# A fused two-layer graph network: order of steps in the joined projection stage, and the queues of its loads and stores

## The chip, the cores and the metric

One core of a Trainium2 chip. The metric is the device time of one execution in microseconds. A core has five engines with a queue each: TensorE (matmul), VectorE, ScalarE, GpSimd and SyncE, which here only gives out DMAs. They are ordered against each other by semaphores alone.

## The reference, cut to what matters

Two layers over 3125 nodes of 256 features and 50000 edges. The stage concerned ends the first layer and prepares the second:

```python
x = x + _L0_ffn_ref(_layernorm(x))            # two experts per node, weighted, layer-normed
xn = _layernorm(x)
x = x + _L1_gnn_ref(xn, edge_index, ...) + _L1_mix_ref(xn, ...)
# gnn: x_lin = xn @ W; a_src, a_dst = two scores per head and node; softmax over the edges of a node
# mix: rmsnorm(xn), q, k, v = x @ w_qkv; q, k = elu(.) + 1; kv = sum over nodes of k (outer) v
```

## The kernel before

Nodes lie on 125 lanes, 25 to a lane, and are worked on as 25 tiles of 125 nodes, in five groups of five tiles (`TB`, `NB`). The kernel is a row of stages with a barrier of all engines between them. The diff touches one, `stage_project1`. Two things run through it.

First the combination of the experts' rows, on VectorE for a whole group at a time: `weigh` (L1719) adds the two gathered expert rows of a node with their weights, `measure_y` and `centre_y` (L1727, L1735) norm the sum, `add_y` (L1741) adds it to x, `measure_x`, `spread_of_x` and `scales` (L1746 to L1765) give the factors of the second norm. ScalarE takes two roots (`root`, `two_roots`) and writes the normed rows (`normalise`, L1659). Each root and each following exponential needs another function table, so ScalarE loads one.

Then the projection, `project(u)` (L1674 on ScalarE, L1775 on VectorE, loop L1898 on TensorE): TensorE transposes the group's rows (L1887), ScalarE copies them (L231, L232), TensorE makes the queries of the group (L1894), VectorE and ScalarE apply the activation (L1780, L1678, L1791), and for each tile TensorE makes key and value (L1907) and the graph features and scores (L1912), VectorE the low part and the key (`low_part`, `key_of`), ScalarE the copies and the exponential (`keep_tile`), TensorE adds to the state (L1878). Products of two tiles can wait in PSUM. The steps of the next group's combination stand between those of this group's tiles in the order that VectorE's `project` and ScalarE's `project` write out by hand.

SyncE stores each finished tile of features (L1615). GpSimd gathers the expert rows (L1640, 50 of them), scatters the last 91 of 391 columns of edge records to memory (L245 by L1645), waits for them to land and tells SyncE, which loads the sorted records back (L1617). When the scores are shifted by their least value, SyncE stores them twice (L1620 into the table's rows, L1621 by node). VectorE masks the state into `kvz`, clears the accumulator `sums1` of the next stage (L1863) and converts the records' first column (L1865). The next stage, `stage_edges1`, starts with GpSimd's gathers by those records (L2112) and the load of the scores (L2095).

`sums1` lies in the same memory as the gathered expert rows; the last reading of those is the weighing of the last group.

Of the kernel before, what the change touches and what calls it, by code (L numbers as in the profile page):

```python
# [17 lines left out]
P = 128  # L18

NN = 3125  # L20
NP = 125
# [3 lines left out]
H = 4  # L25
# [4 lines left out]
EVEN = 112  # L30
# [13 lines left out]
W1 = HD + 1  # L44
# [183 lines left out]
def keep_transposed(act, sem, xT, ps):  # L228

    flat = xT.rearrange("p t c n -> p (t c n)")  # L230
    act.activation(flat[:, 0:4 * DC * NP].rearrange("p (b n) -> p b n", b=2), ps[:, 0:2, 0:2 * DC * NP], ACT.Copy)  # L231
    act.activation(flat[:, 4 * DC * NP:], ps[:, 2, 0:DC * NP], ACT.Copy).then_inc(sem, 1)  # L232
# [1276 lines left out]
def stage_project1(nc, a, k):  # L1509


    with ExitStack() as ctx:
# [67 lines left out]
        s_l = m.sem("least_steps")  # L1580
        s_lT = m.sem("least_turned")
        s_sc = m.sem("score_rows")
        s_land = m.sem("records_landed")
        s_rec = m.sem("records_in")
        s_v = m.sem("vector_steps")
        block = ctx.enter_context(nc.Block(no_gpsimd_drain=True))
# [7 lines left out]
        @block.sync  # L1594
        def _(sp):
            for j, name in enumerate(("L1_gnn_att_src", "L1_gnn_att_dst")):
                sp.dma_start(att[:, j, :], a[name].rearrange("h o -> (h o)").partition_broadcast(P)).then_inc(s_w, 16)
            load_weight(sp, w[:, :, 3 * D:4 * D], a["L1_gnn_W"], s_w)
            for c in range(DC):
                sp.dma_start(n1[:, c:c + 1], a["L1_mix_w_norm1"][c * P:(c + 1) * P].rearrange("(p a) -> p a", a=1)).then_inc(s_w, 16)  # L1600
            load_weight(sp, w[:, :, 0:3 * D], a["L1_mix_w_qkv"], s_w)
            sp.dma_start(gamma[:], a["L0_ffn_gamma"].partition_broadcast(NP)).then_inc(s_w, 16)
            load_weight(sp, k["wout_p1"], a["L1_mix_w_out"], s_w)
            for t, name in ((k["n2"], "L1_mix_w_norm2"), (k["bout_p1"], "L1_mix_b_out"), (k["gbias"], "L1_gnn_bias")):
                sp.dma_start(t, a[name].partition_broadcast(NP)).then_inc(s_w, 16)

            sp.wait_ge(s_z, 1)
            extra = B1 * G1_BINS - NN
            sp.dma_start(k["table1"][NN:B1 * G1_BINS, :], zrow[0:extra, :]).then_inc(s_zero, 16)
            sp.dma_start(k["score1"][NN:, :], zrow[0:extra, 0:2 * H]).then_inc(s_zero, 16)  # L1610
            sp.dma_start(k["table1"][B1 * G1_BINS:, :], zrow[:]).then_inc(s_zero, 16)
            to = k["table1"][0:NN, :].rearrange("(p t) d -> p t d", p=NP)
            for t in range(TN):
                sp.wait_ge(s_vxk, t + 1)
                sp.dma_start(to[:, t, 0:H * W1], lin[:, t % TB, :]).then_inc(s_tab, 16)  # L1615
            sp.wait_ge(s_land, 1)
            sp.dma_start(k["rec"][:, 0:G1_N, :].rearrange("p t f -> p (t f)"),  # L1617
                         k["sorted1"][0:P * G1_N, :].rearrange("(p t) f -> p (t f)", p=P)).then_inc(s_rec, 16)
            sp.wait_ge(s_sc, 1)
            sp.dma_start(to[:, :, H * W1:], score[:, :, 0:H]).then_inc(s_zero, 16)  # L1620
            sp.dma_start(k["score1"][0:NN, :].rearrange("(p t) d -> p t d", p=NP), score[:]).then_inc(s_zero, 16)  # L1621
            sp.wait_ge(s_w, 16 * 11)
            sp.wait_ge(s_zero, 80)
            sp.wait_ge(s_tab, 16 * TN)

        @block.gpsimd
        def _(pool):
            nc.gpsimd.memset(same[:], 1.0).then_inc(s_same, 1)
            view = same[:].rearrange("p (h d) -> p h d", h=HC)
            pool.wait_ge(s_same, 1)  # L1630
            nc.gpsimd.affine_select(out=view, in_=view, compare_op=ALU.is_ge, fill=0.0, base=0,
                                    pattern=[[-MD, HC], [0, MD]], channel_multiplier=1).then_inc(s_same, 1)
            pool.wait_ge(s_same, 2)
            nc.gpsimd.affine_select(out=view, in_=view, compare_op=ALU.is_ge, fill=0.0, base=MD - 1,
                                    pattern=[[MD, HC], [0, MD]], channel_multiplier=-1).then_inc(s_same, 1)

            for u in range(NB):
                for t in columns(u):
                    for r in range(TOPK):
                        pool.indirect_dma_start(  # L1640
                            out=yk[:, r, t, :], out_offset=None, in_=k["expert_out"],
                            in_offset=bass.IndirectOffsetOnAxis(ap=k["pairs"][:, r * TN + t:r * TN + t + 1].bitcast(U32), axis=0)
                        ).then_inc(s_y[u], 16)

            scatter_records(pool, k["sorted1"], k["row1"], k["record1"], k["s_scat1"], SCATTERS_EARLY, EC)  # L1645
            scatters_landed(pool, k["s_scat1"])
            pool.sem_inc(s_land, 1)

        @block.scalar
        def _(act):  # L1650
            def root(u):
                act.wait_ge(s_var[0], u + 1)
                nc.scalar.activation(var[:, 0, group(u)], var[:, 0, group(u)], ACT.Sqrt, bias=k["eps5"][0:NP, :]).then_inc(s_std[0], 1)
# [5 lines left out]
            def normalise(u):  # L1659
                act.wait_ge(s_back, u + 1)  # L1660
                for j, t in enumerate(columns(u)):
                    last = nc.scalar.activation(rows[:, t, :], x[:, t, :], ACT.Identity, scale=unroots[:, u, 1, j:j + 1], bias=back[:, t:t + 1])
                last.then_inc(s_xn, 1)
# [10 lines left out]
            def project(u):  # L1674
                act.wait_ge(s_xT, u + 1)
                keep_transposed(nc.scalar, s_xTk, xT[:], ps_T)
                act.wait_ge(s_lowq, u + 1)
                nc.scalar.activation(lowq[:], lowq[:], ACT.Exp).then_inc(s_expq, 1)  # L1678
                for j, t in enumerate(columns(u)):
                    if j == 0 and u:  # L1680
                        act.wait_ge(s_tab, u * 16 * TB)
                    if u:
                        act.wait_ge(s_kv, t - TB + 1)
                    keep_tile(t, j)
                    if j == 1 and u + 1 < NB:
                        root(u + 1)
                    if j == 3 and u + 1 < NB:
                        two_roots(u + 1)
                if u + 1 < NB:
                    normalise(u + 1)  # L1690

            act.wait_ge(s_w, 16 * 11)
            for c in range(DC):
# [9 lines left out]
        def _(dve):  # L1703
# [71 lines left out]
            def project(u):  # L1775
                n = u + 1
                more = n < NB
                dve.wait_ge(s_q, n)
                for bank, at, size in SPANS:
                    last = v.tensor_scalar(lowq[:, at:at + size], ps_T[:, bank, 0:size], 0.0, None, ALU.min)  # L1780
                last.then_inc(s_lowq, 1)
                if more:
                    weigh(n, 0)
                t = u * TB
                if u:
                    dve.wait_ge(s_kv, t)
                low_part(t, 0)
                dve.wait_ge(s_expq, n)
                for c, t0, size, bank, at in PIECES:
                    begin = SPANS[bank][1] + at  # L1790
                    last = v.scalar_tensor_tensor(qT[:, t + t0:t + t0 + size, c, :],  # L1791
                                                  ps_T[:, bank, at:at + size * NP].rearrange("p (t n) -> p t n", t=size), 0.0,
                                                  lowq[:, begin:begin + size * NP].rearrange("p (t n) -> p t n", t=size), ALU.max, ALU.add)
                last.then_inc(s_qT, 1)
                key_of(t, 0)
                if more:
                    weigh(n, 1)
                low_part(t + 1, 1)
                if more:
                    measure_y(n)  # L1800
                key_of(t + 1, 1)
                low_part(t + 2, 2)
                if more:
                    centre_y(n)
                key_of(t + 2, 2)
                if more:
                    add_y(n)
                low_part(t + 3, 3)
                if more:
                    measure_x(n)  # L1810
                key_of(t + 3, 3)
                if more:
                    spread_of_x(n)
                low_part(t + 4, 4)
                if more:
                    scales(n)
                key_of(t + 4, 4)

            o.done(v.memset(val[:], 1.0))
            v.memset(zrow[:], 0.0).then_inc(s_z, 1)  # L1820
# [39 lines left out]
            for c in range(DC):  # L1860
                o.done(v.tensor_tensor(kvz[:, c, 0:P], kvs_of[c][:, 0:P], same[:], ALU.mult))
                o.done(v.tensor_scalar(kvz[:, c, P:], heads, kvs_of[c][:, P:], None, ALU.mult))
            o.done(v.memset(k["sums1"], 0.0))  # L1863
            dve.wait_ge(s_rec, 16)
            o.done(v.tensor_copy(k["rec"][:, 0:G1_N, 0].bitcast(I32), k["rec"][:, 0:G1_N, 0]))  # L1865

# [1058 lines left out]
```

## Time and profile before

| | us |
|---|---|
| median of 3 runs | 2845.75 (2844.44 to 2851.44) |
| profiled execution | 2843.54 |
| its span | 2841.8 |

Engine busy time over the span, from the page:

```profile
PE 1659.2 (58%) x12361; PEld 1202.8 (42%) x12362; DVE 1835.1 (65%) x5560; ACT 850.7 (30%) x2657; POOL 1814.0 (64%) x1828
```

PE is TensorE, PEld its weight load, DVE VectorE, ACT ScalarE, POOL GpSimd, and SP (SPq) SyncE. A line of the profile names the line of the kernel, the engine, the operation and what it writes and reads. The stage lies between 1620 and 1836.5 us of the span.

### The profile page before, as it was taken

What the parts mean: (1) busy time and instruction counts of PE and PEld (TensorE: products, weight loads), DVE (VectorE), ACT (ScalarE), POOL (GpSimd) and SP (SyncE); (2) the same over time, 40 slices, a digit from 0 to 9 for tenths busy, and PEclk for the clock granted to TensorE, in tenths of its full rate; (3) what the DMA queues carried; (4) which work ended last, traced back from release to release, by engine and by line L of the source; (5) the groups of instructions that cost most, each with busy time, mean ns of one, the idle gap of its engine ahead of it and who ended that gap; (6) DMA issues with size and microseconds to landing.
All of it is one profiled execution on the core that took longest, in us unless ns stands there. A gap on an engine that the chain in (4) does not pass through costs nothing. (4 is left out here: it accounts for less than half of the span.)

```text
span 2841.8 us, 52033 instructions
## 1 busy us (share of the span) xinstructions
PE 1659.2 (58%) x12361; PEld 1202.8 (42%) x12362; DVE 1835.1 (65%) x5560; ACT 850.7 (30%) x2657; POOL 1814.0 (64%) x1828
## 2 busy tenths in 40 slices
PE   0488444236666666424999657655666655401997
PEld 0254333124444454312666434344555544301665
DVE  8776699568777777621222256488888888865322
ACT  0144111024444444101333234323333333301231
POOL 3777777757777777777777777377777777600000
PEclk9999666568888888657999878767666676655998
DMA  7000000053333333042333330233333337321000
GB/s 225 9 22 20 2 2 1 1 197 105 107 107 107 107 106 106 21 168 89 86 87 86 100 90 21 46 106 106 105 106 106 106 106 150 82 69 58 10 18 18
DMA packets 169775, 224.90 MB, mean 79 GB/s; under 512 B 77731, under 2 KB 129226, under 8 KB 169513
## 3 DMA queue, kind: packets, MB, share of 16 engines
q0 software_dynamic: 74368, 138.96, 18.3%
q1 hardware_dynamic: 95270, 84.55, 10.4%
q14 instruction: 105, 0.86, 0.1%
q8 instruction: 32, 0.52, 0.1%
HBM read 184.08 MB, written 39.29 MB: 79 GB/s over the span
## 5 line engine op out<-in xcount | busy, mean ns | idle before, releaser
L2112 POOL DMA_INDIRECT e_rows<-mid_table,rec x488 | 486.1, 996 | 184.1 <-issue 137.7
L245 POOL DMA_INDIRECT mid_sorted<-p_record,p_row x391 | 414.0, 1059 | 159.7 <-issue 122.2
L922 POOL DMA_INDIRECT e_rows<-mid_table,e_rec x440 | 420.0, 954 | 150.4 <-issue 91.4
L245 POOL DMA_INDIRECT mid_sorted<-keep_record,keep_row x391 | 393.7, 1007 | 129.4 <-issue 121.1
L1084 PE MATMUL e_ps_A<-e_rows,e_hot 128*125 128x260 f32 x880 | 306.5, 481 | 0.0
L2374 ACT ACTIVATE room<-room 128x66 f32 x488 | 126.1, 258 | 260.7 <-ACT room L2374 209.8
L1084 PEld LDWEIGHTS e_ps_A<-e_rows,e_hot 128*125 128x125 f32 x880 | 188.0, 237 | 25.1
L1069 PE MATMUL e_ps_T<-e_identb,e_hot 128*125 128x128 bf16 x446 | 84.7, 279 | 185.0 <-DVE e_hot L945 184.0
L1443 DVE COPY x_hidden<-x_ps_h 128x512 f32<-128x512 f32 x64 | 44.3, 692 | 220.3 <-PE x_ps_h L1472 220.3
L2439 PE MATMUL e_ps_mT<-keep_ident,room 128*128 128x128 f32 x488 | 118.2, 423 | 116.4 <-DVE room L2136 116.4
L965 DVE TENSOR_TENSOR e_rows<-e_rows 128x512 f32<-128x512 f32 x220 | 150.8, 685 | 1.8 <-ACT e_rows L1049 1.4
L2439 PEld LDWEIGHTS e_ps_mT<-keep_ident,room 128*128 128x128 f32 x488 | 95.8, 223 | 126.4 <-issue 126.2
L1069 PEld LDWEIGHTS e_ps_T<-e_identb,e_hot 128*125 128x125 bf16 x446 | 50.4, 159 | 206.0 <-DVE e_hot L945 205.2
L1472 PE MATMUL x_ps_h<-w,x_xT 128*128 x256 | 127.8, 622 | 15.4 <-ACT x_xT L1421 15.1
L2163 DVE SCALAR_TENSOR_TENSOR room<-room,e_scale,e_ps_A 128x65 f32<-128x65 f32 x488 | 135.6, 278 | 0.7 <-issue 0.2
L1488 PE MATMUL x_ps_y<-x_w,x_hT 128*128 x512 | 122.4, 382 | 1.6 <-ACT x_hT L1428 1.6
L1041 ACT ACTIVATE acc<-e_state 125x260 f32 x220 | 92.4, 420 | 97.8 <-DVE e_state L973 97.1
L142 DVE TENSOR_TENSOR_SCAN p_running<-p_ones,p_first,p_mask 128x391 f32<-128x391 f32 (+1 forms) x125 | 116.4, 994 | 5.3 <-DVE p_mask L139 5.3
L836 PE MATMUL p_ps_mix<-p_kw,p_qvT 128*125 128x256 f32 x100 | 50.1, 655 | 119.5 <-DVE keep_x L748 118.5
L945 DVE TENSOR_SCALAR e_hot<-keep_iota,e_rec 128x125 f32<-128x125 f32 x446 | 117.0, 375 | 1.1
L1488 PEld LDWEIGHTS x_ps_y<-x_w,x_hT 128*128 128x128 f32 x512 | 95.8, 189 | 44.8 <-issue 30.7
L2811 PE MATMUL f_ps_h<-f_xT,f_w 128*128 (+2 forms) x320 | 99.2, 459 | 20.5 <-DVE f_w L2746 12.4
(526 smaller groups left out, 4023.9 us busy)
## 6 DMA issues: line engine op xcount, KB each, us to landing
mid_expert_in<-p_zrow SPq DMA_DIRECT2D x1, 8192.0 KB
w<-in_L_ffn_w SPq DMA_DIRECT2D x16, 512.0 KB
x_w<-in_L_ffn_w SPq DMA_DIRECT2D x16, 512.0 KB
x_xs<-mid_expert_in SPq DMA_DIRECT2D x64, 128.0 KB
x_b<-in_L_ffn_b SPq DMA_DIRECT2D x64, 128.0 KB
mid_expert_out<-x_y SPq DMA_DIRECT2D x64, 128.0 KB
e_rows<-mid_table,rec POOLq DMA_INDIRECT x488
e_rows<-mid_table,e_rec POOLq DMA_INDIRECT x440, 2.8
```

The lines of the kernel that those rows point to most:

```text
L245: pool.indirect_dma_start(out=to, out_offset=bass.IndirectOffsetOnAxis(ap=row[:, t:t + 1].bitcast(U32), axis=0), in_=record[:, t, :], in_o ...
L922: pool.indirect_dma_start(out=rows[:, s % RING * 2 + j, :], out_offset=None, in_=k["table"], in_offset=bass.IndirectOffsetOnAxis(ap=rec[:, ...
L945: last = nc.vector.tensor_scalar(hot[:, q * 2 + j, :], k["iota"][:, 0:NP], rec[:, bass.ds(s * 2 + j, 1), 1:2].rearrange("p a b -> p (a b)" ...
L965: nc.vector.tensor_tensor(r, r, spread(w, P, 2, H, HD), ALU.mult).then_inc(s_wm, 1)
L1069: last = nc.tensor.transpose(ps_T[q % 2][0:NP, j, 0:P], halves[:, :, 1], identb[:])
L1084: last = nc.tensor.matmul(ps_A[0:NP, q % 4, 0:ROW], hot[:, q * 2 + j, :], rows[:, q * 2 + j, :], start=j == 0, stop=j == 1)
L1472: last = nc.tensor.matmul(ps_h[q % 2][:], xT[:, q % 2, c, :], k["w1"][:, bass.ds(e, 1), c, :].rearrange("p a f -> p (a f)"), start=c == 0, ...
L1488: last = nc.tensor.matmul(ps_y[q % 2][:], hT[:, c, :], w2[:, bass.ds(e, 1), c, :].rearrange("p a d -> p (a d)"), start=c == 0, stop=c == F ...
L2112: pool.indirect_dma_start(out=rows[:, j, q, :], out_offset=None, in_=k["table1"], in_offset=bass.IndirectOffsetOnAxis(ap=rec[:, i * TG + q ...
L2163: v.scalar_tensor_tensor(state[:, j, q, 0:W1], before, scale[:, j, q:q + 1], sums_of(j)[:, q // HALF, q % HALF * W1:(q % HALF + 1) * W1], ...
L2374: nc.scalar.activation(acc[:, bass.ds(block_of, 1), :].rearrange("p a w -> p (a w)"), state[:, j, q, :], ACT.Copy).then_inc(s_keep, 1)
L2439: last = nc.tensor.transpose(ps_mT[:, q // HALF, q % HALF * P:(q % HALF + 1) * P], marked[:, q, :], k["ident"][:])
```

## The change

VectorE's `project(u)` weighs and measures the next group before it waits for this group's queries, and spreads the other steps between the tiles, each one or two places earlier than before. ScalarE's `project(u)` takes the first root right after the copies of the transposes, the two other roots after tile 2 instead of 3, and normalises after tile 3 instead of 4. In the last group, which has no next one, the accumulator is cleared in three parts between the last tiles. The records are loaded by GpSimd's queue, behind its own wait for the scatters. Each score store becomes two, lanes 0 to 111 and 112 to 124.

```diff
-            sp.wait_ge(s_land, 1)
-            sp.dma_start(k["rec"][:, 0:G1_N, :].rearrange("p t f -> p (t f)"),
-                         k["sorted1"][0:P * G1_N, :].rearrange("(p t) f -> p (t f)", p=P)).then_inc(s_rec, 16)
             sp.wait_ge(s_sc, 1)
-            sp.dma_start(to[:, :, H * W1:], score[:, :, 0:H]).then_inc(s_zero, 16)
-            sp.dma_start(k["score1"][0:NN, :].rearrange("(p t) d -> p t d", p=NP), score[:]).then_inc(s_zero, 16)
+            for rows_ in (slice(0, EVEN), slice(EVEN, NP)):
+                sp.dma_start(to[rows_, :, H * W1:], score[rows_, :, 0:H]).then_inc(s_zero, 16)
+            by_node = k["score1"][0:NN, :].rearrange("(p t) d -> p t d", p=NP)
+            for rows_ in (slice(0, EVEN), slice(EVEN, NP)):
+                sp.dma_start(by_node[rows_], score[rows_]).then_inc(s_zero, 16)
             sp.wait_ge(s_w, 16 * 11)
-            sp.wait_ge(s_zero, 80)
+            sp.wait_ge(s_zero, 112)
...
             scatters_landed(pool, k["s_scat1"])
-            pool.sem_inc(s_land, 1)
+            pool.dma_start(k["rec"][:, 0:G1_N, :].rearrange("p t f -> p (t f)"),
+                           k["sorted1"][0:P * G1_N, :].rearrange("(p t) f -> p (t f)", p=P)).then_inc(s_rec, 16)
...
                 keep_transposed(nc.scalar, s_xTk, xT[:], ps_T)
+                more = u + 1 < NB
+                if more:
+                    root(u + 1)
...
                     keep_tile(t, j)
-                    if j == 1 and u + 1 < NB:
-                        root(u + 1)
-                    if j == 3 and u + 1 < NB:
+                    if j == 2 and more:
                         two_roots(u + 1)
-                if u + 1 < NB:
-                    normalise(u + 1)
+                    if j == 3 and more:
+                        normalise(u + 1)
...
                 more = n < NB
+                if more:
+                    weigh(n, 0)
+                    weigh(n, 1)
+                    measure_y(n)
                 dve.wait_ge(s_q, n)
...
-                if more:
-                    weigh(n, 0)
                 t = u * TB
                 if u:
                     dve.wait_ge(s_kv, t)
                 low_part(t, 0)
+                if more:
+                    centre_y(n)
                 dve.wait_ge(s_expq, n)
...
                 key_of(t, 0)
-                if more:
-                    weigh(n, 1)
                 low_part(t + 1, 1)
                 if more:
-                    measure_y(n)
+                    add_y(n)
                 key_of(t + 1, 1)
                 low_part(t + 2, 2)
                 if more:
-                    centre_y(n)
+                    measure_x(n)
+                    spread_of_x(n)
+                else:
+                    clear(0)
                 key_of(t + 2, 2)
-                if more:
-                    add_y(n)
                 low_part(t + 3, 3)
                 if more:
-                    measure_x(n)
+                    scales(n)
+                else:
+                    clear(1)
                 key_of(t + 3, 3)
-                if more:
-                    spread_of_x(n)
                 low_part(t + 4, 4)
-                if more:
-                    scales(n)
+                if not more:
+                    clear(2)
                 key_of(t + 4, 4)
+
+            def clear(n):
+                size = G1_BINS * (W1 + 1) // 3
+                o.done(v.memset(k["sums1"][:, n * size:(n + 1) * size], 0.0))
...
-            o.done(v.memset(k["sums1"], 0.0))
             dve.wait_ge(s_rec, 16)
```

## Rows read from the trace of the kernel before

**Rows 1.** Stretches: bounds, length, PE, PEld, DVE, ACT, POOL busy; clock, DMA, GB/s.

```profile
1669.50:1805.80 136.30, 103.07 (x345) 66.18 (x344) 80.97 (x268) 67.24 (x136) 100.92 (x103) 0.85 0.13 33
1805.80:1825.10 19.30, 16.56 (x65) 10.21 (x64) 8.62 (x23) 7.20 (x21) 0.00 (x0) 0.97 0.20 60
1729.00:1733.00 4.00, 3.50 (x11) 2.55 (x11) 0.00 (x0) 1.27 (x2) 3.08 (x4) 0.50 0.02 1
```

**Rows 2.** Waits, 1640 to 1860 us: who, for whom, us in total, times, longest.

```profile
DVE p_lowq L1780 <- PE p_ps_T L1894: 58.1, 5, 12.9
...
SPq L1624 <- DMA mid_score<-p_score: 3.7, 1, 3.7
```

**Rows 3.** Timeline, seam of groups 0 and 1; last row next seam: start, us, what.

```profile
1689.17 0.46 ACT L1667 ACTIVATE p_lin<-p_ps_v,keep_rms 125x256 f32<-125x256 f32 x1
...
1691.68 2.55 ACT L1662 ACTIVATE acc<-keep_x,p_back,p_unroots 125x256 f32<-125x256 f32 x5
...
1694.29 2.35 PE L1887 MATMUL p_ps_T<-keep_ident,acc 125*128 125x125 f32 x10 [5.25 <-ACT acc L1662]
...
1698.00 4.49 PE L1894 MATMUL p_ps_T<-p_xT,w_p 128*128 128x375 f32 x16 [0.50 <-ACT p_xT L232]
...
1702.52 1.59 DVE L1780 TENSOR_SCALAR p_lowq<-p_ps_T 128x375 f32<-128x375 f32 x3 [10.28 <-PE p_ps_T L1894]
...
1731.18 6.49 PE L1894 MATMUL p_ps_T<-p_xT,w_p 128*128 128x375 f32 x16 [0.50 <-ACT p_xT L232]
```

**Rows 4.** Groups of VectorE by line, 1640 to 1860 us: busy, mean ns, idle.

```profile
L1739 DVE SCALAR_TENSOR_TENSOR acc<-acc,p_mean,p_gamma 125x256 f32<-125x256 f32 x25 | 10.2, 474 | 0.0
...
L1791 DVE SCALAR_TENSOR_TENSOR q_room<-p_ps_T,p_lowq 128x375 f32<-128x375 f32 (+1 forms) x20 | 8.2, 474 | 0.7 <-ACT p_lowq L1678 0.7
```

**Rows 5.** Timeline: group 0's combination, and two keys of the last group.

```profile
1641.43 4.17 DVE L1725 SCALAR_TENSOR_TENSOR acc<-room,keep_gate,acc 125x256 f32<-125x256 f32 x10 [0.16 <-DVE w_p L1828]
...
1648.12 0.17 DVE L1733 SCALAR_TENSOR_TENSOR p_var<-p_tmp,p_var 125x5 f32<-125x5 f32 x1
...
1815.42 0.42 DVE L1773 SCALAR_TENSOR_TENSOR p_key<-p_ps_p,p_low 125x256 f32<-125x256 f32 x1 [1.77 <-ACT p_val L1672]
...
1818.47 0.42 DVE L1773 SCALAR_TENSOR_TENSOR p_key<-p_ps_p,p_low 125x256 f32<-125x256 f32 x1 [1.77 <-ACT p_val L1672]
```

**Rows 6.** Timeline: GpSimd's last gather and last scatter, and the stage's end.

```profile
1683.62 1.05 POOL L1640 DMA_INDIRECT room<-mid_expert_out,keep_pairs  x1 [0.31 <-issue]
...
1800.55 0.96 POOL L245 DMA_INDIRECT mid_sorted<-keep_record,keep_row  x1 [0.30 <-issue]
...
1825.11 0.92 SPq L1620 DMA_DIRECT2D mid_table<-p_score  x1
...
1826.08 5.60 SPq L1621 DMA_DIRECT2D mid_score<-p_score  x1
1827.31 5.45 DVE L1863 MEMSET room<- 128x6468 f32 x1 [1.29 <-issue]
1832.67 0.35 DVE L1865 CAST rec<-rec 128x488 int32<-128x488 f32 x1
...
1837.18 0.98 POOL L2112 DMA_INDIRECT e_rows<-mid_table,rec  x1 [35.67 <-POOLq L266]
```

**Rows 7.** DMA issues, 1660 to 1870 us: count, KB each, us to landing.

```profile
rec<-mid_sorted SPq DMA_DIRECT2D x1, 488.0 KB, 4.0
```

**Rows 8.** Timeline of an earlier stage: a memset and GpSimd's gathers beside VectorE.

```profile
588.47 5.47 DVE L983 MEMSET acc<- 128x6500 f32 x1 [1.30 <-issue]
...
590.66 0.94 POOL L922 DMA_INDIRECT e_rows<-mid_table,e_rec  x1 [0.30 <-issue]
...
604.41 1.52 POOL L922 DMA_INDIRECT e_rows<-mid_table,e_rec  x1 [0.30 <-issue]
```

**Rows 9.** Stretches within the score store and within the store of attended rows (L2102).

```profile
1829.00:1830.00 1.00, 0.00 (x0) 0.00 (x0) 1.00 (x1) 0.00 (x0) 0.00 (x0) 0.50 0.60 7
...
2515.00:2519.00 4.00, 0.00 (x0) 0.00 (x0) 3.97 (x2) 0.00 (x0) 0.00 (x0) 0.50 0.78 159
```

More of the change, by code:

```diff
@@ L1582, in stage_project1 @@
         s_sc = m.sem("score_rows")
-        s_land = m.sem("records_landed")
         s_rec = m.sem("records_in")
```

## The prediction

> **What bounds the kernel now.** I read first the busy time by stretch [rows 1]. The stage that the diff touches runs from about 1620 to 1836.5 us. Between the starts of the first and the last group's query step lie 136.3 us, 34.1 us for each of four groups, and no engine is full in them: TensorE is busy 103 us, VectorE 81, ScalarE 67. In the last group, which has no next group to prepare, five tiles and the score step take 19.3 us with TensorE busy for 16.6. So the four groups are bound by a chain that passes from engine to engine. The list of waits [rows 2] says where it breaks: VectorE waited five times, 58.1 us in all, for the query products in front of L1780, up to 12.9 us each. The timeline of a seam between groups [rows 3] shows the chain: ScalarE's copies and exponentials of the last tile (from 1689.17), its normalising (to 1694.24), ten transposes, two copies, 16 query matmuls, and VectorE starts the next group at 1702.52. VectorE has nothing to do in that seam and is at work nearly all the time outside it: 81 us in four groups are 20.2 us in each [rows 1]. The next group's weighing and statistics lie in those 20.2 us, ahead of the seam, though their inputs are there long before.
>
> Behind the last group stand the two score stores [rows 6]: given out at 1825.11 and 1826.08, the second one held in issue for 5.60 us, and SyncE's last wait is for it, 3.7 us after its issue ended [rows 2], so until 1835.4. The next stage's first gather starts at 1837.18, 1.8 us later. VectorE's memset and conversion end at 1833.02 and are not on this path, nor is the load of the records.
>
> **The change, part by part.** (a) Weighing and `measure_y` of the next group move into the seam. Their price stands in the first group, where they already lie side by side: from 1641.43 to 1648.29, 6.9 us [rows 5]. The seam holds 10.3 us or more [rows 3], so they are nearly hidden, and the tile phase loses 6.9 us of VectorE. I lay out one group from the start of L1780 (zero). On VectorE: L1780 1.6, first low part 0.4, `centre_y` 2.2 (10.2 us for five groups, and a reciprocal of 0.2), four query pieces 1.6 (8.2 for five), key 0.4: the first key ends at 6.3 [rows 3 to 5]. TensorE waited for it and then runs three tile steps of 3.05 us, the distance between two keys of the last group [rows 5], less the last state product: tile 3's value product ends at about 13.0. VectorE keeps up: `add_y` (2.1) ends at 8.7 and key 1 at 9.0, when TensorE needs it near 9.7; `measure_x` and `spread_of_x` (2.7 as `measure_y` from 1645.6 on, and two small instructions more, 3.1) end at 12.4 and key 2 at 12.8, when TensorE needs it at 13.0. ScalarE then does tile 3's copies, a table load, exponential, copy and the normalising in one run, as before for tile 4: 1689.17 to 1694.24, 5.1 us [rows 3]. That ends at 18.1. Transposes, copies and queries follow as before, 8.3 us to the next L1780 [rows 3]: 26.4. VectorE's own chain ends just there: key 4 comes after ScalarE's normalising and 1.3 us of tile 4's work, at 19.8, plus 6.9 is 26.7. I take 26.7.
>
> Two waits are new in place. ScalarE waits in `root` for the statistics, with the exponential of the query part and tile 0's copies queued behind; but that exponential waits for L1780, which stands behind the same statistics on VectorE, so only the reload of its table (1.3 us) could show, and L1780's own 1.6 us covers it. Then `normalise` stands ahead of tile 4's copies; behind those waits key 4 alone, counted above. The number of table loads is the same. The weighing needs the expert rows of the next group; the last of the 50 gathers starts at 1683.62 and they come every 1.25 us, so the 20th, the last for group 1, starts near 1646 [rows 6]; VectorE comes to it near 1656, behind group 0's own preparation. Cost nothing; if one came late, only that seam would grow.
>
> The size of the seam depends on TensorE's clock. The query matmuls took 4.49 us in one seam and 6.49 in another, where the granted clock was 0.50, its level of 1.2 GHz, after 5 us in which TensorE had no work [rows 1, 3]. The new seams leave it idle for 1.3 us instead of 5.2. I take 27.5 us per group, about half a dip, with 26.7 (no dip) and 28.7 (each time) as ends. Four groups: 110 instead of 136.3, so the last L1780 comes at 1779.5 (1776.3 to 1784.3) instead of 1805.8.
>
> (b) The memset of 5.45 us becomes three of about 1.8 us between keys of the last group. VectorE idles 1.77 us there for ScalarE [rows 5], and TensorE needs the key about 1 us later still. Before the memset stand 1.29 us of issue [rows 6]; if each third had that, I would pay up to 1.0 us in all. I take 0.3. What it saved lay under the score stores.
>
> (c) Score stores in four parts. In the old form, 3125 pieces of 16 bytes ran at 7 GB/s, 437 pieces per us, with a DMA share of 0.60 [rows 9]. The nearest rows of many small pieces to memory from a tile of 32 rows per store show 159 GB/s at 256 bytes, 621 pieces per us [rows 9]. By that rate the 3125 pieces save about 1 us, and the second store, which took 3.7 us after its issue, perhaps 1.5. The upper end is that the parts of 112 rows spread over three times as many engines: 10.3 us from first issue to last landing become 4.8. The lower end is no gain and 0.8 us for two more issues. I take minus 2.5: 7.8 us. The Trainium skill, page "DMA: Bandwidth & Descriptors", has two rules here that speak against each other. Under "Why a DMA increments its semaphore by 16 and not by 1" it says that a transfer uses the largest number of engines up to 16 that divides its outermost size, which is 5 for 125 rows and 16 for 112; no view here names the engines. Under "Rules for kernel authors" it calls splitting by partitions pointless; that is the lower end, 11.1 us.
>
> So SyncE's path ends at 1779.5 + 19.3 + 0.3 + 7.8 = 1806.9 (1801 to 1816).
>
> (d) The records. Their scatters are GpSimd's, one each 1.26 us, bound by issue alone, and nothing in the change makes them earlier: the last starts at 1800.55 and ends at 1801.51 [rows 6]. Before, that was 20 us ahead of the load. Now it is not. Landing of the last scatter: another 1.5 us (estimate, gathers took 3.1 from issue to landing). Then the load of 488 KB: 4.0 us from issue to landing on SyncE's queue [rows 7]; GpSimd's queue shows no direct load here, so I take 4.9, one GpSimd issue of 0.95 on top, with 4.0 and 9 as ends. It lands at 1808.0, the conversion takes 0.35 [rows 6]: 1808.4 (1807.4 to 1812.5). This is later than SyncE's 1806.9, so GpSimd's list becomes what ends the stage. Add the same 1.8 us of barrier: first gather at 1810.2 instead of 1837.18.
>
> **Sum.** 27.0 us sooner; the stages behind start in the same state and keep their length. The profiled execution took 2843.54 us with a span of 2841.8; the span becomes 2814.8 and its time 2816.5. The median of the three runs is 2.2 us above the profiled one: 2845.75 - 27.0 = 2818.8, say 2819.
>
> **The rivals.**
> First, SyncE's path stays last: a clock dip in each seam and stores that gain nothing. 1784.3 + 19.3 + 0.3 + 10.3 = 1814.2, first gather at 1816.0, gain 21: 2825. For it: two of four old seams had the slow queries. Against: the idle time that went ahead of them is gone.
> Second, GpSimd's queue is a slow loader: 4 us more for the load, 2823. For: no such load in this trace.
> Third, the zeroing holds GpSimd up: its three memsets lie beside scatters, 5.4 us in all, and the stage's end is GpSimd's: 2824. Against: a memset of 6500 columns ran beside gathers that took 0.94 us each, the usual time [rows 8]. The Trainium skill, "SBUF — State Buffer", section "SBUF: two separate sides", warns that VectorE's fast modes keep GpSimd from writing descriptors; by that rule the memset could, and the trace doesn't agree for this one.
> Fourth, the change doesn't do what it says: the weighing waits for something in the seam that I didn't see, and the period stays at 34. Then only the stores gain, 2.5 us: 2843.
> Fifth, slower: VectorE, now busier, slows GpSimd's scatters. Beside a conversion and a subtraction on VectorE one GpSimd issue took 1.52 us instead of 0.95 [rows 8]. If each of the 91 scatters took that, the last would end 52 us later, the first gather would start at about 1862, and the kernel would take 2871. It decides from a mean pace of 1.56 us per scatter instead of 1.26, for then the 27 us are eaten. Against: the same instructions lay beside the scatters before, and few scatters were long.
>
> **How the numbers follow.** Forecast (GpSimd's list last, 27 us) 0.55, first rival 0.23, second 0.09, third 0.06, fourth 0.04, fifth 0.03. A measurement of this kernel can tell 0.3%, 8.5 us, from no change. All but the last two are faster by more: 0.93; within 0.3% 0.04; slower 0.03. The range must take in the second and third rival and the bounds of the first and leaves 1 us for the scatter of medians: 2814 to 2828.
>
> **What would show it.** Right: L1780's successors some 27 us apart; L1725 ten in a row in front of them; VectorE's wait there gone; no L1662 behind tile 4's copies; scatters still ending near 1801.5, and the conversion of the records waiting for the load after the score step; 112-row stores with a higher DMA share. Wrong: a period above 29 us, a wait before a key for a memset, scatters with a mean above 1.3 us, or a next stage that is longer than before.

## The result, and the profile after

| | before | changed kernel |
|---|---|---|
| median, all executions side by side | 2845.1 us (4 runs, 2842.06 to 2851.44) | 2813.83 us (4 runs, 2811.17 to 2816.02) |
| profiled execution, its span | 2843.54, 2841.8 | 2816.02, 2814.3 |
| stage: GpSimd's first instruction to the next stage's first gather | 1620.10 to 1837.18: 217.1 | 1621.10 to 1810.17: 189.1 |

The ratio is 0.9888, with a 95% interval of 0.9873 to 0.9903: some 31 us faster. The median lies 0.2 us under the stated range. The profiled execution, the slowest of its four, came out as forecast: first gather at 1810.17 (forecast 1810.2), span 2814.3 (2814.8), time 2816.02 (2816.5). Part of this is luck: the code ahead of the stage was not changed, and yet in the seven profiles that share it the stage starts anywhere between 1617.2 and 1627.0 us.

Of the 27.5 us between the two spans, 28.0 are in the stage; it starts 1.0 us later, and from the first gather to the end both kernels take the same, 1004.6 and 1004.1 us. Stretches of the changed kernel, columns as in [rows 1]: the four groups, the last group to the first gather, and 30 us in the middle.

```profile
1671.90:1774.19 102.29, 87.50 (x345) 54.86 (x344) 75.07 (x246) 63.73 (x133) 77.98 (x80) 1.00 0.16 42
1774.19:1810.17 35.98, 16.48 (x65) 10.14 (x63) 15.52 (x38) 7.19 (x21) 22.37 (x24) 0.76 0.18 37
1700.00:1730.00 30.00, 24.22 (x96) 15.06 (x95) 24.50 (x79) 19.34 (x42) 22.85 (x24) 1.00 0.12 29
```

Four groups took 136.3 us before [rows 1] and take 102.3 now, 25.6 each. The same 345 matmuls count 87.5 us instead of 103.1, and the granted clock is 1.00 instead of 0.85.

A clock of 1.00 throughout is the best case. Each of the other seven profiles with the new order has one fall to 0.50, and their four groups take 103.9 us. The second profile of the changed kernel, its four groups and then the stretch of the fall:

```profile
1675.91:1779.77 103.86, 89.17 (x345) 55.72 (x344) 74.97 (x247) 63.73 (x133) 79.17 (x82) 0.98 0.16 42
1735.10:1738.40 3.30, 3.30 (x7) 1.88 (x6) 2.55 (x8) 0.00 (x0) 2.38 (x4) 0.50 0.06 14
```

TensorE was busy for 1.40 of the 2 us ahead of the fall and all through it, and the group that holds it took 27.4 us instead of 25.8. Why it falls there is open.

Timeline of the changed kernel, the seam (passage) from group 0 to group 1; it answers to [rows 3]. The last numbers are the idle time before an instruction and what ended it.

```profile
1686.98 2.55 ACT L1662 ACTIVATE acc<-keep_x,p_back,p_unroots 125x256 f32<-125x256 f32 x5
1687.12 0.42 DVE L1774 SCALAR_TENSOR_TENSOR p_key<-p_ps_p,p_low 125x256 f32<-125x256 f32 x1 [1.95 <-ACT p_val L1672]
...
1689.59 1.29 PE L1894 MATMUL p_ps_T<-keep_ident,acc 125*128 125x125 f32 x10 [1.28 <-ACT acc L1662]
...
1690.65 0.42 DVE L1774 SCALAR_TENSOR_TENSOR p_key<-p_ps_p,p_low 125x256 f32<-125x256 f32 x1 [2.78 <-ACT p_val L1672]
...
1690.99 4.16 DVE L1726 SCALAR_TENSOR_TENSOR acc<-room,keep_gate,acc 125x256 f32<-125x256 f32 x10
...
1692.24 4.49 PE L1901 MATMUL p_ps_T<-p_xT,w_p 128*128 128x375 f32 x16 [0.40 <-ACT p_xT L232]
...
1697.80 0.17 DVE L1734 SCALAR_TENSOR_TENSOR p_var<-p_tmp,p_var 125x5 f32<-125x5 f32 x1
...
1697.88 1.58 DVE L1785 TENSOR_SCALAR p_lowq<-p_ps_T 128x375 f32<-128x375 f32 x3
1698.00 0.30 ACT L1653 ACTIVATE p_var<-p_var,keep_eps 125x5 f32<-125x5 f32 x1 [4.51 <-DVE p_var L1734]
```

ScalarE normalises (L1662) ahead of tile 4's copies. TensorE has nothing for 1.28 us instead of 5.25, and the ten transposes behind it take 1.29 us instead of 2.35. VectorE no longer waits for the queries: they end at 1696.73, 1692.24 and 4.49 us. Its own weighing and statistics end last, at 1697.97, and L1785 (the old L1780) follows them without idle time. So VectorE's own list now sets the period here, and in the next two seams, where L1785 has no idle time either. In the last seam, where no group is left to weigh, it waits for the queries again (5.69 us, first line below).

Timeline of the changed kernel, last group and the stage's end; it answers to [rows 6].

```profile
1774.19 1.59 DVE L1785 TENSOR_SCALAR p_lowq<-p_ps_T 128x375 f32<-128x375 f32 x3 [5.69 <-PE p_ps_T L1901]
...
1782.43 1.85 DVE L1825 MEMSET room<- 128x2156 f32 x1 [0.40 <-issue]
...
1785.48 1.85 DVE L1825 MEMSET room<- 128x2156 f32 x1 [0.40 <-issue]
...
1793.80 2.20 SPq L1617 DMA_DIRECT2D mid_table<-p_score  x2
...
1796.05 0.97 SPq L1620 DMA_DIRECT2D mid_score<-p_score  x2
...
1801.72 0.96 POOL L245 DMA_INDIRECT mid_sorted<-keep_record,keep_row  x1 [0.30 <-issue]
1804.42 0.58 POOL L1646 DMA_DIRECT2D rec<-mid_sorted  x1 [1.74 <-DMA mid_sorted<-keep_record,keep_row]
1808.18 0.41 DVE L1872 CAST rec<-rec 128x488 int32<-128x488 f32 x1 [13.48 <-DMA rec<-mid_sorted]
...
1810.17 0.99 POOL L2119 DMA_INDIRECT e_rows<-mid_table,rec  x1 [5.16 <-POOLq L266]
```

SyncE's last wait, and the load of the records with the us from its issue to its landing; they answer to [rows 2] and [rows 7].

```profile
SPq L1623 <- DMA mid_score<-p_score: 3.9, 1, 3.9
```

```profile
rec<-mid_sorted POOLq DMA_DIRECT2D x1, 488.0 KB, 3.7
```

SyncE has given out its last store at 1797.0 and waits 3.9 us for it: it is done at 1800.9. The records' conversion ends at 1808.59. So GpSimd's list (last scatter, its landing, the load) ends the stage, 7.7 us behind SyncE.

### The profile page after: what moved, and what is told of

Read it like the earlier page. It is cut to its first block and busy times, and to the rows that moved or that the text cites. A ratio compares the mean times of both kernels' runs of the same rounds, so it can differ in the third digit from the quotient of the medians.

```text
span 2814.3 us, 52035 instructions
## 1 busy us (share of the span) xinstructions
PE 1643.7 (58%) x12361; PEld 1189.6 (42%) x12362; DVE 1836.2 (65%) x5562; ACT 847.6 (30%) x2655; POOL 1812.5 (64%) x1829
## 5 line engine op out<-in xcount | busy, mean ns | idle before, releaser
L922 POOL DMA_INDIRECT e_rows<-mid_table,e_rec x440 | 420.8, 956 | 150.7 <-issue 90.5
L1084 PEld LDWEIGHTS e_ps_A<-e_rows,e_hot 128*125 128x125 f32 x880 | 190.6, 240 | 25.8
L142 DVE TENSOR_TENSOR_SCAN p_running<-p_ones,p_first,p_mask 128x391 f32<-128x391 f32 (+1 forms) x125 | 116.5, 993 | 5.3 <-DVE p_mask L139 5.3
```

Source lines behind the costliest of these rows:

```text
L922: pool.indirect_dma_start(out=rows[:, s % RING * 2 + j, :], out_offset=None, in_=k["table"], in_offset=bass.IndirectOffsetOnAxis(ap=rec[:, ...
L1084: last = nc.tensor.matmul(ps_A[0:NP, q % 4, 0:ROW], hot[:, q * 2 + j, :], rows[:, q * 2 + j, :], start=j == 0, stop=j == 1)
```

## The experiments

The stage's length below is always that of the table above, from the profiled execution. Each ratio is to the kernel before on the same chip.

**The order alone.** The whole stores, the memset at the end and SyncE's load of the records stay as before. Against the changed kernel:

```diff
+            sp.wait_ge(s_land, 1)
+            sp.dma_start(k["rec"][:, 0:G1_N, :].rearrange("p t f -> p (t f)"),
+                         k["sorted1"][0:P * G1_N, :].rearrange("(p t) f -> p (t f)", p=P)).then_inc(s_rec, 16)
             sp.wait_ge(s_sc, 1)
-            for rows_ in (slice(0, EVEN), slice(EVEN, NP)):
-                sp.dma_start(to[rows_, :, H * W1:], score[rows_, :, 0:H]).then_inc(s_zero, 16)
+            sp.dma_start(to[:, :, H * W1:], score[:, :, 0:H]).then_inc(s_zero, 16)
...
-                else:
-                    clear(0)
...
+            o.done(v.memset(k["sums1"], 0.0))
```

> The stage length below is the time from the stage's first GpSimd instruction to the next stage's first gather: 217.1 us before the change, 189.1 after it. This kernel has the new order of the combination and of ScalarE's roots, and the rest as before: accumulator cleared at the end, records loaded by SyncE's queue ahead of the score stores, score stores whole. Theory (GpSimd's list of scatters bounds, and SyncE's load of the records waits for it with the score stores queued behind): last scatter lands near 1803 as ever, then the load's issue, then 10.3 us of stores, next gather near 1815.7, stage length about 195, gain 22 us against before. Rival (the time follows the tiles alone, the load waits for nothing): scores are ready near 1793, stores end near 1804 and the stage length is about 184, a larger gain than with the whole change.

Measured: 2822.15 us, ratio 0.993 (0.9915 to 0.9944), stage 196.7 us: 20.4 of the 28.0 us, and 1.7 longer than the 195 expected. The four groups took 103.9 us, as in the changed kernel's second profile, so the new period needs nothing else of the change. Timeline and SyncE's waits of this kernel:

```profile
1807.25 0.96 POOL L245 DMA_INDIRECT mid_sorted<-keep_record,keep_row  x1 [0.30 <-issue]
1809.40 0.35 SPq L1617 DMA_DIRECT2D rec<-mid_sorted  x1
1809.79 0.92 SPq L1620 DMA_DIRECT2D mid_table<-p_score  x1
1810.76 6.89 SPq L1621 DMA_DIRECT2D mid_score<-p_score  x1
```

```profile
SPq L1617 <- POOLq L1647: 14.4, 1, 14.4
```

SyncE stood 14.4 us in the wait for the scatters, until 1809.4. VectorE had finished the scores by 1798.7, so for the last 10.7 us their stores stood queued behind it. Before, that wait cost nothing, because the scatters were over 20 us earlier [rows 6].

**The order, and the load on GpSimd's queue.** Against the kernel of the run above:

```diff
-            sp.wait_ge(s_land, 1)
-            sp.dma_start(k["rec"][:, 0:G1_N, :].rearrange("p t f -> p (t f)"),
...
-            pool.sem_inc(s_land, 1)
+            pool.dma_start(k["rec"][:, 0:G1_N, :].rearrange("p t f -> p (t f)"),
```

> New order and the records loaded by GpSimd's queue; the stores whole and the accumulator cleared at the end as before. Theory (GpSimd's list ends the stage at about 1808): score stores end near 1804 and the clearing near 1801, both under it, so stage length 189, the same as the whole change, within 1 us; the split of the stores and of the clearing is worth nothing here. Rival (SyncE's stores end the stage): 3 to 6 us longer than the whole change, 192 to 195.

Measured: 2816.44 us, ratio 0.9905 (0.989 to 0.992), stage 190.4 us. The timeline:

```profile
1800.68 5.83 SPq L1617 DMA_DIRECT2D mid_score<-p_score  x1
...
1808.18 0.96 POOL L245 DMA_INDIRECT mid_sorted<-keep_record,keep_row  x1 [0.30 <-issue]
1811.65 0.59 POOL L1643 DMA_DIRECT2D rec<-mid_sorted  x1 [2.51 <-DMA mid_sorted<-keep_record,keep_row]
```

Behind the new order, moving the load is worth 6.3 us. No run kept it on SyncE's queue behind the score stores, so what is shown is the worth of taking the wait out from in front of them, and not of GpSimd's queue in itself. The stage is 1.4 us longer than with the whole change, and half of that is the landing of the scatters, 2.51 us here and 1.74 there. The split stores and the three clears show no other gain: here too the stores (done at 1810.5) and the clearing end ahead of the load.

**All but the order.** The old `project` functions of VectorE and ScalarE; clears, load and split stores as changed. Against the changed kernel:

```diff
-                if more:
-                    weigh(n, 0)
-                    weigh(n, 1)
-                    measure_y(n)
                 dve.wait_ge(s_q, n)
+                if more:
+                    weigh(n, 0)
```

> The order of steps as before; the accumulator cleared in three parts between the last tiles, records loaded by GpSimd's queue, score stores split. Theory: the score stores end the stage here. In the changed kernel they took 4.4 us instead of 10.3, so the stage length is 217.1 - 6 = 211, gain 6 us. Rival, my own figure in the prediction (the rate of small pieces hardly changes with the number of engines): minus 2.5, stage length 214.6. If the two halves of the change add up the sum with the order alone is 28, as measured for the whole in the profiles.

Measured: 2839.19 us, ratio 0.999 (0.998 to 0.9999), stage 214.2 us: 2.9 less than before, half of the 6 expected. My own figure in the prediction, here the rival with 214.6, was the better one: the 4.4 us that the expectation gives the changed kernel's stores leave out most of their landing, with which they took 7.1. The timeline and SyncE's wait:

```profile
1824.20 2.26 SPq L1617 DMA_DIRECT2D mid_table<-p_score  x2
...
1826.51 0.96 SPq L1620 DMA_DIRECT2D mid_score<-p_score  x2
```

```profile
SPq L1623 <- DMA mid_score<-p_score: 2.9, 1, 2.9
```

From first issue to last landing the stores took 6.2 us, 4.1 less than the 10.3 of before; the clears took back 0.2, and the stage's head was 0.9 longer. The two parts give 20.4 and 2.9 apart, 23.3, and 28.0 together: by this account the load on GpSimd's queue is worth nothing while SyncE's stores end last (no run moved it alone), and 6 us once the order is changed.

**Is it GpSimd's list?** Eight more of the scatters in this stage and eight fewer in the one before.

```diff
-SCATTERS_EARLY = 300
+SCATTERS_EARLY = 292
```

> The changed kernel with 8 of the scatters of records moved from the stage before into this one (300 to 292), so GpSimd's list here is longer by 8 times 1.26 us = 10.1 us. Theory (GpSimd's list ends the stage): stage length 189.1 + 10.1 = 199.2. The stage before gets at most 1 us shorter, because its end waits for other stores too; in all 8 to 10 us slower than the changed kernel. Rival (the score stores or the tile loop end it): they had 10 us of room at most, so the stage length stays within 1 us of 189.

Measured: 2825.1 us, ratio 0.994 (0.9926 to 0.9954), stage 199.0 us, 9.95 longer; eight scatters at 1.26 us are 10.1. The timeline shows the same end, later:

```profile
1809.04 0.95 POOL L245 DMA_INDIRECT mid_sorted<-keep_record,keep_row  x1 [0.30 <-issue]
1811.73 0.58 POOL L1646 DMA_DIRECT2D rec<-mid_sorted  x1 [1.74 <-DMA mid_sorted<-keep_record,keep_row]
```

Every scatter counts in full, so nothing else ends behind GpSimd's list. The time rose with it: the stage before hardly got shorter (374.7 us from GpSimd's first scatter of expert inputs to this stage, 376.9 and 375.8 in the two profiles of the changed kernel), and GpSimd was idle for 9.58 us at its end.

**The changed kernel again,** on the chip of the next three kernels.

> The changed kernel itself, unaltered, to see what of the difference between 27 us (forecast), 28 (the stage in the two profiles) and 31 to 32 (the medians) is in the stage and what is scatter outside it. Theory (the stage is 28 us shorter and nothing else changed): stage length 189 again, and a gain of 28 us within 2. Rival (something outside the stage gained 3 to 4 us too): a gain of 31 us or more again, and in the profile a stage before or behind it that is 3 us shorter.

Measured: 2816.54 us, ratio 0.9896 (0.9876 to 0.9916), stage 188.7 us. By this ratio the gain is 29.6 us, within the theory's 28 ± 2, but the interval reaches from 24 to 35 us and so takes in the rival too. The profile says more: the stage is 28.4 us shorter than before, what lies behind it is as long as ever (1004.3 us), and it starts later than before and not sooner, at 1625.7.

**Less in front of the scatters.** GpSimd's `same` mask, three instructions ahead of the first gather, moves behind the load of the records.

```diff
-            nc.gpsimd.memset(same[:], 1.0).then_inc(s_same, 1)
-            view = same[:].rearrange("p (h d) -> p h d", h=HC)
...
             pool.dma_start(k["rec"][:, 0:G1_N, :].rearrange("p t f -> p (t f)"),
                            k["sorted1"][0:P * G1_N, :].rearrange("(p t) f -> p (t f)", p=P)).then_inc(s_rec, 16)
+            nc.gpsimd.memset(same[:], 1.0).then_inc(s_same, 1)
+            view = same[:].rearrange("p (h d) -> p h d", h=HC)
...
```

> The changed kernel with GpSimd's making of the mask (L1627 to L1634, 1.1 us) moved from the head of its list in this stage behind its load of the records. Theory (GpSimd's list ends the stage): everything on it comes 1.1 us sooner, the mask is made while the load is under way, VectorE's masking of the state (0.8 us) still ends before the load lands. From the first instruction on GpSimd to the next gather 188.0 instead of 189.1. Rival (the mask now comes too late): VectorE waits for it, and the stage is as long as before or longer by up to 1 us.

Measured: 2816.24 us, ratio 0.9909 (0.9889 to 0.993), stage 187.9 us as expected. A saving of 1 us in the stage can't be seen in the time: the ratio is no better than the changed kernel's.

**Three and six scatters fewer,** on top of that (303, and in the second kernel 306).

```diff
-SCATTERS_EARLY = 300
+SCATTERS_EARLY = 303
```

> As e6, and three scatters of records moved out of this stage into the one before (300 to 303). Theory: this stage 3 times 1.26 = 3.8 us shorter still, 184.2. The stage before pays where GpSimd's list ends it: it was idle at the end of that stage for 3.7 us in the changed kernel's profile and 0.5 in others. So the sum is between minus 4.9 and minus 1.1 us against the changed kernel. Rival (GpSimd's list is the limit in both stages): no gain but the 1.1 of the mask.

> As e6, with six scatters moved into the stage before (300 to 306). Theory: this stage 7.6 us shorter than with e6, 180.4, since the score stores end 7 us before the load of the records in the changed kernel. The stage before becomes longer by 7.6 less GpSimd's idle time at its end (0.5 to 3.7). In all 1 to 5 us faster than the changed kernel, not better than e7 by more than 1 us. Rival (the score stores or the last tiles end this stage first): the stage stops shrinking at about 182.

Measured: 2819.36 us, ratio 0.9922 (0.99 to 0.9944), and 2823.41 us, 0.9923 (0.9904 to 0.9943). The stage took 186.0 and 184.1 us, 1.9 and 3.8 less than without, where 3.8 and 7.6 were expected. The timeline of the kernel with six fewer:

```profile
1805.59 2.20 SPq L1617 DMA_DIRECT2D mid_table<-p_score  x2
1805.94 0.96 POOL L245 DMA_INDIRECT mid_sorted<-keep_record,keep_row  x1 [0.30 <-issue]
1807.84 0.97 SPq L1620 DMA_DIRECT2D mid_score<-p_score  x2
1812.01 0.58 POOL L1637 DMA_DIRECT2D rec<-mid_sorted  x1 [5.10 <-DMA mid_sorted<-keep_record,keep_row]
```

Now the last scatter lies beside the score stores, and its landing takes 5.10 us (2.77 with three fewer, 1.74 where the stores are long done). And what was moved out made the stage before longer, by 3.0 and 7.2 us (measured in the same way) against the kernel with only the mask moved. GpSimd was idle for only 1.19 us at the end of the stage before, so its list stands at the end of both stages, and a scatter moved from one to the other gains nothing: the rival of the first expectation. None of the three versions beats the changed kernel.

## Why the prediction was right, and where it missed

**(a) The order: right, and under-sized.** A group takes 25.6 us in this profile and 26.0 in the seven others with the new order; 27.5 was taken, with 26.7 as the best end. Several terms were too large. The 0.8 us per group for a slow clock were 0 here and some 0.4 in the others: the granted clock is 1.00, its level of 2.4 GHz, with at most one fall in four groups, and no fall reached the queries. They took 4.49 us in every seam, where two of the four seams of before took 6.49 [rows 3] and 6.65. The transposes too had been counted at 2.35 us and took 1.29. And VectorE's chain, which I had put at 26.7, closed at 26.0 in the first seam: key 4 ended 19.2 us after L1785's start instead of 19.8. The chain itself is the one that I laid out: weighing hidden but for 1.1 us, and ScalarE ready at 17.6 us (18.1). The tie of two engines at its end is not there: the queries were done 1.1 us ahead of VectorE. The last seam took 24.7, because nothing is weighed there any more, which I had left out. None of this reached the time, since GpSimd's list ends the stage.

**(b) Clearing: right.** 0.40 us of issue in front of each 1.85 us, the last group 19.6 us instead of 19.3.

**(c) Score stores: the right size, and then beside the point.** 7.1 us in the changed kernel and 6.2 without the new order; 7.8 was taken. The working had an error in it: from 437 to 621 pieces per us, 3125 pieces save 2.1 us and not 1. The pieces then left faster than either rate. Stretches with the 3125 pieces of 16 bytes in them, before and in the changed kernel, and the changed kernel's last 2.9 us up to the end of SyncE's wait:

```profile
1826.50:1832.50 6.00, 0.00 (x0) 0.00 (x0) 5.19 (x1) 0.00 (x0) 0.00 (x0) 0.50 0.55 8
1795.00:1797.50 2.50, 0.00 (x0) 0.00 (x0) 0.00 (x0) 0.00 (x0) 1.89 (x3) 0.50 0.72 37
1798.00:1800.90 2.90, 0.00 (x0) 0.00 (x0) 0.00 (x0) 0.00 (x0) 2.29 (x3) 0.50 0.03 1
```

They took about 6 us before and under 2.5 now, at a higher DMA share, as the sign for a right forecast said. (The second store is only 125 pieces, 800 bytes for each lane.) But in the last 2.9 us almost nothing moves any more, where before the last pieces went out until 1835.0 and the wait was over at 1835.4. So some 2.5 us of the gain were lost again in the landing; why is open. The Trainium skill, page "DMA: Bandwidth & Descriptors", section "Why a DMA increments its semaphore by 16 and not by 1", has a rule that comes to 5 engines for 125 rows and 16 for 112. The measured times agree with it, and not with the advice against splitting under that page's "Rules for kernel authors". That advice gives as its reason that both parts use all 16 engines anyway, which by the first rule a store of 125 rows does not. No view here names the engines.

**(d) The records: right, by terms that cancel.** The last scatter started at 1801.72 instead of 1800.55, mostly because the whole stage began 1.0 us later. Its landing took 1.74 us (1.5). The load took 3.7 us to landing where 4.9 was taken: GpSimd's queue (3.6 to 3.8 us in all its profiles) is no slower a loader than SyncE's (4.0 [rows 7], 3.6 in the run with the order alone). The conversion ended at 1808.59 (1808.4). The step that made this the last path was right, and the run with eight more scatters shows it; SyncE's path, forecast 1.5 us ahead, was 7.7 us ahead. So 7.7 us of what the order gains stay unused behind GpSimd.

**The rivals.** SyncE's path last: false, since both of its conditions failed. SyncE's path does end last if the load stays ahead of the stores on its queue, as the first run shows, but for that reason and not for the rival's. A slow load: false. Zeroing that holds GpSimd up: false, the scatters beside the three memsets took 0.95 to 0.96 us. The Trainium skill, "SBUF — State Buffer", section "SBUF: two separate sides", warns of VectorE's fast modes. It doesn't name a memset, so the prediction stretched it, and the trace shows no delay beside one. Slower scatters: false. The group of GpSimd's scatters in the changed kernel:

```profile
L245 POOL DMA_INDIRECT mid_sorted<-keep_record,keep_row x91 | 88.8, 976 | 27.7 <-issue 27.7
```

Before, the same 91 had a mean of 979 ns.

**What failed: the last line of the sum.** I added 2.2 us to the forecast for the profiled execution, because the median of before was 2.2 above its profiled one. That is no property of the kernel: the changed kernel's median is 2.2 us below its profiled one. This term of +2.2 that measured -2.2 makes 4.4 of the 5.2 us between the forecast of 2819 and the 2813.8 measured. And the range had 1 us for the scatter of medians, while single executions of the kernel before lay between 2836 and 2856 us over all runs. 28 us lie within both intervals of the changed kernel (0.9873 to 0.9903 is 27.6 to 36 us, 0.9876 to 0.9916 is 24 to 35); the profiles account for 28, and I take the rest of the 31 for such scatter, which is not shown.

**Where that scatter is from** can be read in part in the ten profiles. From the first gather behind the stage to the end of the span they take 1002.2 to 1004.6 us, but the first stage, with the same code in all, ends between 580.2 and 591.9 us. Groups of GpSimd's scatters from 75 to 578 us of it, first of the kernel with the mask moved (580.15), then of the one with order and load (591.91):

```profile
L245 POOL DMA_INDIRECT mid_sorted<-p_record,p_row x367 | 380.1, 1036 | 116.0 <-issue 116.0
```

```profile
L245 POOL DMA_INDIRECT mid_sorted<-p_record,p_row x364 | 389.0, 1069 | 115.0 <-issue 115.0
```

33 ns for each of 367 are 12.1 us, against 11.8 between the ends, and the other eight lie between in nearly the same order (1041 ns for 581.7, 1049 for 585.2, 1056 for 586.9, 1065 for 590.4). The timeline of the kernel before shows which are long:

```profile
318.19 1.01 POOL L245 DMA_INDIRECT mid_sorted<-p_record,p_row  x1 [0.30 <-issue]
319.25 3.80 DVE L142 TENSOR_TENSOR_SCAN p_running<-p_ones,p_first,p_mask 128x391 f32<-128x391 f32 x4 [0.18 <-DVE p_mask L139]
319.51 1.54 POOL L245 DMA_INDIRECT mid_sorted<-p_record,p_row  x1 [0.30 <-issue]
321.35 1.54 POOL L245 DMA_INDIRECT mid_sorted<-p_record,p_row  x1 [0.30 <-issue]
```

Beside VectorE's scans (L142) most scatters in this stretch take 1.54 us, elsewhere 0.96 to 1.1, but for 1.35 beside the masked copy that follows each group of scans. How many fall so seems to differ from one execution to the next. This is read from profiles and was not tried: no run changed the scans. So my fifth rival has a likely mechanism, in another stage and for other instructions than those that were moved.

It is not the only source. From the first stage's end to this stage's start the profiles with the same code there take 1033.3 to 1041.3 us; the two of the changed kernel take 1035.9 and 1041.3. In the second of them 423 gathers of the stage behind (L922) took 410.2 us together instead of 403.6; what held them was not looked for.

## What to carry to other kernels

Lay a group out engine by engine, put the next group's preparation where its engine waits anyway, and then ask at once which list ends last, for that one takes the rest of the gain: here GpSimd's. A wait inside a queue that cost nothing can hold finished work back once the rest is faster, so an edit that would gain nothing alone (a load moved to the queue that already waits) may be worth 6 us beside another. And forecast a ratio or a profiled time: the distance between one profile and a median of three or four runs is scatter, and the range needs a few us for it on either side.

## What was not expected of the hardware

Two VectorE instructions on large operands each held one GpSimd scatter until they ended. Timeline of the changed kernel in the gate stage, between the first layer's edges and its experts; the kernel before shows the same 7.33 and 6.54.

```profile
1156.06 6.83 DVE L1201 TENSOR_TENSOR acc<-acc 125x6400 f32<-125x6400 f32 x1
1156.40 7.33 POOL L245 DMA_INDIRECT mid_sorted<-keep_record,keep_row  x1 [0.30 <-issue]
...
1162.92 6.83 DVE L1203 TENSOR_TENSOR keep_x<-keep_x,acc 125x6400 f32<-125x6400 f32 x1
1164.04 6.54 POOL L245 DMA_INDIRECT mid_sorted<-keep_record,keep_row  x1 [0.30 <-issue]
```

Memsets of 2156 and of 6500 columns did not do that (0.95 us in this stage, [rows 8]). The landing of the last scatter was longer beside SyncE's score stores: 1.74 us where they were done, 2.51 and 2.77 where they ended beside it, and 5.10 where they were given out beside it.
